# A plain DMA writes the tables' last rows into every gather slot, and the gathers skip the indices that point there

## The reference

```python
VOCAB = 12500; NF = 26; D = 64; B = 2048
x = dense_inputs
for W, b, g, be in bot:                       # 13 -> 512 -> 256 -> 64
    x = _bn(jax.nn.relu(x @ W + b), g, be)
embs = jax.vmap(lambda tbl, idx: tbl[idx], in_axes=(0, 1), out_axes=1)(emb_tables, sparse_inputs)
T = jnp.concatenate([embs, x[:, None, :]], axis=1)
Z = jnp.einsum('bnd,bmd->bnm', T, T)
R = jnp.concatenate([x, Z[:, iu, ju]], axis=1)
for W, b, g, be in top:                       # 415 -> 512 -> 256 -> 1
    h = _bn(jax.nn.relu(h @ W + b), g, be)
return jax.nn.sigmoid(h)
```

## Time and profile before

| | |
|---|---|
| median of 3 runs | 583.62 us |
| the profiled execution, its own time | 583.09 us |
| its span, first to last instruction | 581.0 us |
| time outside the span | 2.1 us |
| mean granted TensorE clock | 0.762 |
| busy: PE, PEld, DVE, ACT, POOL | 368.5, 278.4, 238.6, 190.0, 396.2 us |
| gathers | 416, 13.66 MB |
| mean busy share of the DMA engines, gathers' queue | 18.2% |

### The profile page before, as it was taken

How to read it: one execution, slowest core, us unless ns; L and a number is a source line. 1 busy time by engine, 2 the same in 40 slices (tenths; PEclk the granted TensorE clock), 3 DMA queues, 4 the chain that set the end, 5 groups by cost and what they waited for, 6 DMA issues and landing times.

```text
span 581.0 us, 13877 instructions
## 1 busy us (share of the span) xinstructions
PE 368.5 (63%) x5806; PEld 278.4 (48%) x5827; DVE 238.6 (41%) x640; ACT 190.0 (33%) x509; POOL 396.2 (68%) x426
## 2 busy tenths in 40 slices
PE   6959768678678282735637281735637281767895
PEld 2328437466477161533526171533535170656682
DVE  5772354644634242424223242424234142453622
ACT  4742145425325050413214050413213050454223
POOL 5777777777777777777777777777777777771100
PEclk9999888687587666685859576575859575788998
DMA  8212122222222122222122221212222221220000
GB/s 245 53 26 28 25 29 28 28 29 28 30 28 28 27 28 29 29 27 29 25 29 30 27 29 26 29 27 28 30 29 27 28 27 26 30 27 9 2 0 1
DMA packets 15895, 18.30 MB, mean 31 GB/s; under 512 B 7614, under 2 KB 8894, under 8 KB 15695
## 3 DMA queue, kind: packets, MB, share of 16 engines
q0 software_dynamic: 13312, 13.66, 18.2%
q1 hardware_dynamic: 2524, 3.72, 1.9%
HBM read 17.34 MB, written 0.01 MB: 30 GB/s over the span
## 4 chain that ended last, share of the span: by engine, by line
POOL 66%; issue 22%; PE 7%; DVE 2%; ACT 2%; DMA 1%; POOLq 0%; DVEq 0%; ACTq 0%
POOL emb L320 63%; POOL emb L331 3%; PE l_bank L393 3%; PE l_bank L399 1%; PE l_bank L507 1%; ACT Zs L280 1%; DMA emb<-table,stage 0%; DVE moments_top L743 0%; PE l_bank L554 0%; DMA idx_raw<-idx 0%; PE l_bank L504 0%; PE tr_bank L479 0%; ACT prob L699 0%; DVE stats_t L872 0%; ACT norm_top L588 0%
## 5 line engine op out<-in xcount | busy, mean ns | idle before, releaser
L320 POOL DMA_INDIRECT emb<-table,stage x390 | 369.3, 947 | 121.6 <-issue 118.5
L280 ACT ACTIVATE Zs<-z_bank 27x112 f32<-27x112 f32 (+3 forms) x272 | 92.3, 339 | 209.6 <-PE z_bank L455 203.9
L441 PE MATMUL tr_bank<-ident,emb 128*128 128x128 f32 x195 | 39.7, 331 | 138.6 <-DMA emb<-table,stage 115.2
L254 DVE COPY Zs<-z_bank 27x112 f32<-27x112 f32 (+3 forms) x272 | 88.8, 326 | 47.9 <-PE z_bank L455 42.8
L469 PE MATMUL l_bank<-Zs,tw_sb 128*128 128x128 f32 x840 | 106.2, 279 | 0.0
L469 PEld LDWEIGHTS l_bank<-Zs,tw_sb 128*128 128x128 f32 x840 | 101.9, 197 | 0.0
L853 DVE COPY TT<-tr_bank 128x512 f32<-128x512 f32 (+1 forms) x60 | 55.7, 972 | 108.4 <-PE tr_bank L441 108.0
L441 PEld LDWEIGHTS tr_bank<-ident,emb 128*128 128x128 f32 x195 | 25.7, 162 | 151.0 <-issue 104.7
L455 PE MATMUL z_bank<-TT 64*27 64x26 f32 x3840 | 59.9, 220 | 30.6 <-issue 19.3
L455 PEld LDWEIGHTS z_bank<-TT 64*27 64x27 f32 x3840 | 54.4, 137 | 38.4 <-issue 36.1
L864 DVE BATCH_NORM_STATS2 stats_t<-h_part 128x128 f32 x60 | 17.7, 295 | 111.3 <-ACT hidden_hi L648 111.3
(11 more groups left out here) (120 smaller groups left out, 276.0 us busy)
## 6 DMA issues: line engine op xcount, KB each, us to landing
emb<-table,stage POOLq DMA_INDIRECT x416, 2.7
tw_sb<-tw0x SPq DMA_DIRECT2D x1, 1792.0 KB, 8.7
bw_sb<-bw SPq DMA_DIRECT2D x1, 512.0 KB
tw_sb<-tw SPq DMA_DIRECT2D x1, 512.0 KB, 11.5
twx_sb<-twx SPq DMA_DIRECT2D x1, 256.0 KB, 9.7
idx_raw<-idx SPq DMA_DIRECT2D x1, 169.0 KB, 2.8
bw_sb<-bw SPq DMA_DIRECT2D x2, 64.0 KB
hidden<-dense_t SPq DMA_DIRECT2D x1, 104.0 KB
```

The lines of the kernel that those rows point to most:

```text
L254: last = copy(dst, src[:, :, ZC * q:ZC * q + w])
L280: return nc.scalar.activation(dst, src, ACT.Copy)
L320: pool.indirect_dma_start(out=emb[:, s, k, h, :], out_offset=None, in_=table, in_offset=bass.IndirectOffsetOnAxis(ap=stage[:, s, col:col + ...
L441: tr = nc.tensor.transpose(tr_bank[g % 2][:, c * P:(c + 1) * P], emb[:, s, k, :, :].rearrange("p h d -> p (h d)"), ident[:, :])
```

## The change

A new input, top_rows, holds for every partition the last rows of the tables that the partition serves, once in the layout of the loop's slots and once in that of the last part. SyncE copies it into a slot (128 partitions by 1664 numbers, 832 KB) before the slot's gathers: for slot 0 as the second DMA of the queue, for slots 1 and 2 behind the loads of the weights, then for each further part when slot_open allows it, and once in the last part's layout. Each such copy increments a semaphore filled, for which POOL waits before the part's first gather.

VectorE now gives an index at or above 12499 the number 4194304 (SKIPPED) in place of 12499, one operation more for each of the two blocks. Every gather gets the bound 324999, the stacked tables' last row, with the rule that an index above it moves nothing and is no error.

```diff
+TOP_ROW = VOCAB - 1
+SKIPPED = 1 << 22
...
             sp.dma_start(idx_raw[:, FIRST_COLS], idx[:, FIRST_COLS]).then_inc(first_idx_loaded, 16)
+            sp.dma_start(emb[:, 0, :, :, :].rearrange("p k h d -> p (k h d)"), top_rows[0]).then_inc(filled[0], 16)
             sp.dma_start(idx_raw[:, LATER_COLS], idx[:, LATER_COLS]).then_inc(idx_loaded, 16)
...
+            for s in range(1, SLOTS):
+                sp.dma_start(emb[:, s, :, :, :].rearrange("p k h d -> p (k h d)"), top_rows[0]).then_inc(filled[s], 16)
+            with sp.Fori(0, LOOPS - 1) as it:
+                for s in range(SLOTS):
+                    sp.wait_ge(slot_open, it * SLOTS + (SLOTS + s + 1))
+                    sp.dma_start(emb[:, s, :, :, :].rearrange("p k h d -> p (k h d)"),
+                                 top_rows[0]).then_inc(filled[s], 16)
+            sp.wait_ge(slot_open, PARTS)
+            sp.dma_start(emb[:, LAST_SLOT, :, :, :].rearrange("p k h d -> p (k h d)"),
+                         top_rows[1]).then_inc(filled[LAST_SLOT], 16)
             sp.wait_ge(prob_ready, 1)
...
                     pool.wait_ge(slot_open, it * SLOTS + (s + 1))
+                    pool.wait_ge(filled[s], it * 16 + 16)
                     pool.sem_inc(part_started, 1)
...
                                 in_offset=bass.IndirectOffsetOnAxis(ap=stage[:, s, col:col + 1], axis=0),
+                                bounds_check=NF * VOCAB - 1, oob_is_err=False,
                             ).then_inc(landed[s][k // GROUP], 16)
...
             pool.wait_ge(slot_open, PARTS)
+            pool.wait_ge(filled[LAST_SLOT], (LOOPS + 1) * 16)
...
-                step(nc.vector.tensor_scalar(idx_clamped[:, cols], idx_wrapped[:, cols], 0.0, float(VOCAB - 1),
-                                             ALU.max, ALU.min))
+                step(nc.vector.tensor_scalar(idx_skip[:, cols], idx_wrapped[:, cols], float(TOP_ROW), float(SKIPPED),
+                                             ALU.is_ge, ALU.mult))
+                step(nc.vector.scalar_tensor_tensor(out=idx_clamped[:, cols], in0=idx_wrapped[:, cols],
+                                                    scalar=float(TOP_ROW), in1=idx_skip[:, cols],
+                                                    op0=ALU.min, op1=ALU.max))
```

More of the change, by code:

```diff
@@ L92, in quadrant_columns, with rec_program @@
     return min(ZC, NF - ZC * q)
-def rec_program(nc, idx, table, dense_t, params, identity, bw0, bw1, bw2, tw0x, twx, tw1, out):
+def rec_program(nc, idx, table, top_rows, dense_t, params, identity, bw0, bw1, bw2, tw0x, twx, tw1, out):
     ctx = ExitStack()
@@ L110, in rec_program @@
         idx_wrapped = sb("idx_wrapped", [P, PARTS * PW])
+        idx_skip = sb("idx_skip", [P, PARTS * PW])
         idx_clamped = sb("idx_clamped", [P, (PARTS + SLOTS) * PW])
@@ L184, in rec_program @@
         part_started = sem("part_started")
+        filled = [sem("filled%d" % s) for s in range(SLOTS)]
         landed = [[sem("landed%d_%d" % (s, g)) for g in range(GROUPS)] for s in range(SLOTS)]
@@ L979 @@
         tw0x[QUAD * q + n, c] = w0[D + row]
+    table = get("L0_rec_emb_tables")
+    rows = table[:, TOP_ROW, :].reshape(TP, 2, 1, D)
+    top_rows = np.stack([np.broadcast_to(rows, (TP, 2, 2, D)).transpose(1, 0, 2, 3),
+                         np.broadcast_to(rows, (TP, 2, 2, D)).transpose(1, 2, 0, 3).reshape(2, TP, 2, D)])
+    top_rows = np.repeat(top_rows.reshape(2, 2, TP * 2 * D), UNIT, axis=1)
     arrays = {
         "idx": np.ascontiguousarray(idx),
-        "table": get("L0_rec_emb_tables").reshape(NF * VOCAB, D),
+        "table": table.reshape(NF * VOCAB, D),
+        "top_rows": np.ascontiguousarray(top_rows),
         "dense_t": np.ascontiguousarray(dense_t),
```

## The result

The changed kernel takes **607.36 us** (median of 4 runs, 606.75 to 609.2) against 583.5 before: a ratio of 1.0418 over all single executions, 95% interval 1.0403 to 1.0432 (the two medians alone give 1.0409). It is 4.2% slower. The profiled execution took 607.38 us with a span of 605.6.

The account below looks back on a forecast made before the run. POOL's time per gather, 416 times, was taken as the bound. After a wait for slot 0's copy, 338 gathers from 93.0 us at 1.0785 us end at 457.5; the tail of 58.4 gives 516 us, range 474 to 645.

Parts of the forecast that it names:

- What bounds the kernel: On POOL: only its time for one gather counts, 416 times, one per 1.2515 us; TensorE is second.
- The floor of 482 us: Rival, 13%: rows are all and the test nearly free, gathers of 317 ns, TensorE then bounds at 482 us.
- What skipping saves: In each POOL gather: 74.1% of rows skipped, at up to 6.6 ns a row, saves 627 of 944 ns.
- What the bound costs: In each POOL gather: comparing each index adds 454 ns, the time of a POOL elementwise pass over 128 columns.
- my net of 173 ns: Per POOL gather: 944 - 627 + 454 = 771 ns, 0.173 us less, for a period of 1.0785 us.
- The gap: Between POOL's gathers: stays at 0.30 us despite the bound's register; at most 29 us in all if uncovered.
- The start: Copy into slot 0 ahead of POOL's first gather: it starts at 6.4 us, not 4.36, +2.0 us; TensorE 3 us later.
- The slots: At part 3, POOL waits 2.5 us for slot 0's copy, until 93.0 us; later copies hide.
- The rival with the hardly changed gather: Rival, 20%: fixed setup in each gather, rows and test add almost nothing; 585 us, up to 602 with +40 ns.
- The dear test: Rival, 28%: the test inside each gather costs more than skipping saves, 140 ns net, 643 us; 774 with nothing saved.
- the small gain: Rival, 5%: a time between the bounds, 575 to 584 us.
- My own test in the prediction: In POOL's profile: if kept rows set the time, gathers of tables 20 and 21 last about 0.74 us longer; equal means fixed setup.

Follow-up runs that it names:

- the first run on the late start: Changed kernel with parts 0 to 2 gathered with clamped indices, the three start copies left out and SyncE's queue raising their semaphores: 607.84 us, ratio 1.0405.

## Why the prediction was wrong

I forecast 516 us and got 607.36. The time lies in the range of 474 to 645, but on the other side of no change.

**What bounds the kernel: right.** POOL's gathers, one per period, set the end in every run (from the last gather's end to the end it was 57.0 to 59.7 us in all of them); 416 times the change of a gather plus the change of the start gives each profiled time within 1.5 us (2.6 for the first run on the late start). Where TensorE would take over was never reached: with 16 rows the period was still 1.15 us, above the 0.98 I had worked out. The floor of 482 us stays untested.

**What skipping saves: the step that failed.** I took 846 ns as work by row, since the gather's duration was flat and "128 rows are the only amount I see that is larger than a memset's". I called that a weak reason, and it was. Asked for fewer rows, the gather saves 0.64 to 1.17 ns a row and not 6.6. Worse, a skipped row isn't a row not asked for: it saves 0 (997 ns at 128, 33 and 0 kept). My term of 627 ns was 0. With 74.1% of 128 rows, even a true saving at the measured slopes would have been 61 to 111 ns.

**What the bound costs: over-sized.** 454 ns by the nearest row of POOL, measured 53. The pass over 128 columns was no guide to 128 tests. With 0 saved, which my range had, and the measured 53 paid, the sum is 585.1 + 416 x 0.053 = 607.1. That this meets 607.36 so closely is partly luck, since the start came 1.5 us later than in that sum and the tail was 1.0 shorter. The two errors partly cancelled in my net of 173 ns and would have hidden each other if only the net had been looked at; the runs with the bound alone and with all skipped part them.

**The gap: right.** The register moves are there, 29 ns each, and the gap is 0.30.

**The start: right in kind, small by 1.5 us.** The copies' median to landing is 5.3 us, as interpolated (5.2), but the first copy, issued at 1.20 us, let POOL start at 7.90 and not at 6.4: probably because it shares the engines with the loads issued right behind it; no run tested that. Over the runs with that copy the first gather starts between 6.6 and 7.9 us. TensorE's first transposes came at 81.50, forecast 80.5.

**The slots: the times right, the wait not reached.** Slot 0 opened at 88.75 us (forecast 87.8) and the last packet of its copy ended at 92.86 (forecast 93.0), but POOL, slower and not faster, came to part 3 only at 110.12 and didn't wait. The copies were hidden from POOL as argued, and the gathers at 944 ns beside them show it. They weren't hidden from TensorE, which I had put at nothing: from the first multiplications of part 0 to those of part 4 a part took it 23.1 us, 21.9 before. In a floor case that would have counted.

**The rivals.** The rival with the hardly changed gather named the right mechanism, a fixed setup that rows hardly add to, and ended at 602 with 40 ns for the test; 53 ns end 5 us above it. It had 20%. The dear test (28%) has the sign right, since 53 ns paid are more than 0 saved, but neither of its sizes: it has 140 ns net and 643 us, and its sign was gathers over 1080 ns. Between the 602 of the one and the 643 of the other no case of mine stood, and the result fell there. The Trainium skill ("DMA: Bandwidth & Descriptors", Anatomy of one DMA), which says that many descriptors can be emitted before the incremental cost shows, speaks for it, and the trace agrees with about 1 ns a row in some 830 fixed. I gave the flat duration more weight than that rule, though a flat duration speaks for fixed work as much as for 128 equal pieces. The other figure, also from the Trainium skill ("GPSIMD Engine Reference", Performance versus the Vector engine), 12 cycles for a data-dependent branch, isn't what a bounded gather pays: 53 ns over 128 indices are at most 0.4 ns each, with 0 or 128 of them skipped.

In the chances, I counted 2 of the small gain's 5 in 100 as faster; between 575 and 584 us, with 582.3 as the limit, it would be about 4, so faster had some 0.51.

My own test in the prediction settles it in the first trace with a bound: the gathers of tables 20 and 21 are no longer than their neighbours.

## What to carry to other kernels

When the issue of a gather is the bound, count gathers, not rows or bytes: here some 830 of 944 ns are paid for the instruction, and taking away 73% of the bytes gave nothing. A bound is not free: 43 to 53 ns a gather here, and 53 over 416 are 22 us. Before building the machinery around a cheap instruction (copies, semaphores, an input), measure the instruction by itself in the old kernel: the bound alone was one argument more on two calls and showed 3.7% of the 4.2%.

No run that gathers all the rows it needs beats the kernel before; the three that took less, 545.68, 561.97 and 569.16 us, leave rows out. Fewer gathers with more rows each weren't run, so what one would take isn't known.

## What the runs showed of the hardware beyond that

- A skipped row leaves the structure of a gather as it is: 32 packets each with 128, 33 or 0 rows moved, only their bytes go (13.66, 3.72, 0.24 MB). The count says nothing of POOL's work, for it is 13312 too where 64 or 16 rows are asked for. The landing gets a little shorter, 2.8, 2.4 and 2.1 us (medians).
- Copies of 832 KB beside the gathers don't slow POOL (944 ns with them), but TensorE's issue time before its 256 short multiplications a part went from 1.3 to 2.7 us a part (19.3 / 15, 40.1 / 15), and fell back to 1.5 with the copy issued after them. Blocks of instructions come by DMA and start later beside the copy (3.6 against 1.4 us after the part's first multiplication). In a kernel where TensorE is the bound, that would count.
- Making an index over the bound an error costs 16 ns more than skipping it silently, though no index was over it.
